# Two key products moved between the transposes ahead of the router, and both key weight halves centred back to back on GpSimd

## What is computed

```python
# layer 0: sigmoid attention
s = einsum('bdn,bdm->bnm', Q, K) / sqrt(dk);  x = x + einsum('bvn,bnm->bvm', V, sigmoid(s))
# layer 0: mixture of 16 experts on y = layernorm(x)
logits = y @ router_weight.T + router_bias          # top 4, softmax, scores
gate_up = einsum('th,ehd->etd', y, gate_up_proj)    # then glu, down_proj, weighted sum
# layer 3: keys of the cross attention, from the context alone
kx, vx = split(einsum('bsi,oi->bso', cond, w_kv_x));  kx = _ln(kx.reshape(b, sc, g, d), kxln_w, kxln_b)
```

## Time and profile before

| | before |
|---|---|
| median of 3 runs (lowest, highest) | 1119.61 us (1118.5, 1120.48) |
| the profiled execution's own time | 1118.99 us |
| its span, first to last instruction | 1117.2 us |
| PE busy | 1016.7 us, 91% |
| DVE busy | 875.7 us, 78% |
| ACT busy | 619.3 us, 55% |
| POOL busy | 571.6 us, 51% |
| mean granted TensorE clock | 0.965 of full speed |

### The profile page before, as it was taken

One profiled execution on the slowest core, in us unless ns is written; L12 is line 12 of the kernel. 1 busy time (PEld: TensorE's weight loads), 2 busy tenths in 40 slices (PEclk: granted clock), 3 DMA queues, 4 the chain that ended last, 5 costly groups with the idle time before them and its releaser, 6 DMA issues.

```text
span 1117.2 us, 18801 instructions
## 1 busy us (share of the span) xinstructions
PE 1016.7 (91%) x6432; PEld 862.2 (77%) x6432; DVE 875.7 (78%) x2156; ACT 619.3 (55%) x1646; POOL 571.6 (51%) x416
## 2 busy tenths in 40 slices
PE   6999999999996899878678999999999999999966
PEld 5458888888885686555456888998889888999955
DVE  6348777767768856598999898888897888888773
ACT  1584444444432345677647667765767676666721
POOL 3146666677552232043346675656555655555550
PEclk9899999999997899898879999999999999999998
DMA  7003111011000011000000101010100000000201
GB/s 263 1 1 109 47 40 57 29 58 57 29 1 27 1 55 54 24 1 1 20 1 20 57 1 38 2 57 1 38 2 27 32 20 20 1 21 1 77 1 38
DMA packets 14719, 37.14 MB, mean 33 GB/s; under 512 B 1488, under 2 KB 6688, under 8 KB 14112
## 3 DMA queue, kind: packets, MB, share of 16 engines
q1 hardware_dynamic: 14624, 35.93, 9.5%
HBM read 34.88 MB, written 1.05 MB: 32 GB/s over the span
## 4 chain that ended last, share of the span: by engine, by line
PE 67%; DVE 19%; ACT 6%; issue 4%; POOL 2%; SPq 1%; DMA 1%; DVEq 0%; ACTq 0%; POOLq 0%
PE bank L725 15%; PE bank L747 8%; PE bank L2129 7%; PE bank L2152 7%; PE bank L2062 7%; PE bank L2037 3%; ACT y L2277 3%; PE bank L2073 3%; PE bank L1101 3%; DVE g_ql L1996 2%; PE bank L2051 1%; PE bank L515 1%; DVE bst L241 1%; PE bank L516 1%; PE bank L1116 1%
## 5 line engine op out<-in xcount | busy, mean ns | idle before, releaser
L2277 ACT ACTIVATE y<-bank,g_mx 128x256 f32<-128x256 f32 x256 | 117.2, 484 | 97.1 <-DVE g_mx L2440 97.1
L2559 POOL TENSOR_TENSOR y<-y,g_sm 128x1024 f32<-128x1024 f32 x64 | 120.1, 1896 | 23.8 <-DVE g_sm L2453 23.8
L2535 POOL TENSOR_TENSOR g_c<-arena 128x1024 fp32r<-128x1024 f32 x30 | 64.0, 2135 | 115.2 <-DVE arena L2374 115.2
L2152 PE MATMUL bank<-arena 128*128 128x256 f32 x512 | 116.1, 380 | 0.0
L776 ACT ACTIVATE arena<-arena 128x512 f32<-128x512 f32 x64 | 40.4, 633 | 120.6 <-DVE arena L861 120.5
L2152 PEld LDWEIGHTS bank<-arena 128*128 128x128 f32 x512 | 95.0, 190 | 11.9 <-issue 0.2
L725 PE MATMUL bank<-b_yh,b_wh 128*128 128x512 f32 x256 | 100.7, 393 | 0.0
L725 PE MATMUL bank<-b_yl,b_wh 128*128 128x512 f32 x256 | 100.0, 391 | 0.0
L725 PE MATMUL bank<-b_yh,b_wl 128*128 128x512 f32 x256 | 99.8, 390 | 0.0
L2037 PE MATMUL bank<-cst,y 128*128 128x128 f32 x512 | 73.3, 275 | 17.6 <-DVE x L2362 14.4
L812 POOL TENSOR_TENSOR b_hl<-arena,b_hh 128x512 fp32r<-128x512 f32 x64 | 81.3, 1291 | 9.6 <-ACT b_hh L785 9.6
(11 more groups left out here) (384 smaller groups left out, 3137.2 us busy)
## 6 DMA issues: line engine op xcount, KB each, us to landing
arena<-in_dram SPq DMA_DIRECT2D x37, 512.0 KB, 3.5
arena<-in_dram SPq DMA_DIRECT2D x17, 256.0 KB, 3.7
arena<-in_dram SPq DMA_DIRECT2D x3, 1024.0 KB, 4.8
arena<-in_dram SPq DMA_DIRECT2D x2, 704.0 KB, 7.2
x<-in_dram SPq DMA_DIRECT2D x4, 256.0 KB, 5.3
cx<-in_dram SPq DMA_DIRECT2D x4, 256.0 KB, 5.3
cxT<-in_dram SPq DMA_DIRECT2D x4, 256.0 KB, 5.9
cx<-in_dram SPq DMA_DIRECT2D x1, 1024.0 KB, 6.9
```

Source lines behind the costliest of these rows:

```text
L2152: m = pe.matmul(o[:, st * 256:st * 256 + 256], g_t[:, c, st * P:st * P + P], keys, start=True, stop=True)
L2277: m = act.activation(g_p[:, c, st, :], o[:, st * 256:st * 256 + 256], ACT.Exp, bias=g_mx[j % 2][:, 2 * c + st:2 * c + st + 1], accum_out=g ...
L2535: pool.tensor_tensor(cat, g_o[j % 2], g_om, ALU.subtract).then_inc(s_gc, 1)
L2559: pool.tensor_tensor(pf, pf, sums, ALU.mult).then_inc(s_gp, 1)
```

## The change

On PE key product 0 now stands between the transposes of batches 0 and 1, and key product 1 between those of batches 1 and 2; logits(0) follows the transposes of batch 2 directly, and the rest of the order stays. On ACT the emptying of key product 0 comes ahead of the copy of batch 2's transposes; the copy of logits(0) moves behind the copy of batch 3, and the rounding of the first expert's weights ahead of the emptying of key product 2. On POOL the two centrings stand back to back, and the root for batch 1 comes behind both. Nothing is computed that was not computed before, and nothing is left out.

```diff
@@ -670,10 +670,12 @@
 
             pe.wait_ge(s_cst, 16)
             pe.wait_ge(s_small, 32)
-            yt_pe(pe, K_B, "B", range(3))
+            yt_pe(pe, K_B, "B", (0,))
+            K_raw_pe(pe, 0)
+            yt_pe(pe, K_B, "B", (1,))
+            K_raw_pe(pe, 1)
+            yt_pe(pe, K_B, "B", (2,))
             logits(0)
-            K_raw_pe(pe, 0)
-            K_raw_pe(pe, 1)
             yt_pe(pe, K_B, "B", (3,))
             K_raw_pe(pe, 2)
             logits(1)
@@ -752,14 +754,15 @@
                 o = take(act, ("B", "lgT", h))
                 empty(act.copy(b_sT[0:NE, h * 512:h * 512 + 512], o[0:NE, :]), ("B", "lgT", h))
 
-            yt_act(act, "B", range(3))
+            yt_act(act, "B", range(2))
+            K_raw_act(act, 0)
+            yt_act(act, "B", (2,))
             split_y_act(act, 0)
-            logits(0)
-            K_raw_act(act, 0)
             K_raw_act(act, 1)
             yt_act(act, "B", (3,))
+            logits(0)
+            split_e_act(act, 0)
             K_raw_act(act, 2)
-            split_e_act(act, 0)
             logits(1)
             K_raw_act(act, 3)
             split_y_act(act, 1)
@@ -2963,9 +2966,8 @@
             ln_pool(pool, C, K_A, EPS)
             ln_pool(pool, C, K_B, EPS, batches=(0,))
             K_centre_pool(pool, 0)
-            ln_pool(pool, C, K_B, EPS, batches=(1,))
             K_centre_pool(pool, 1)
-            ln_pool(pool, C, K_B, EPS, batches=(2, 3))
+            ln_pool(pool, C, K_B, EPS, batches=(1, 2, 3))
             B_pool(pool, C)
             M_pool(pool, C)
             G_pool(pool, C)
```

## The result

The changed kernel takes 1113.87 us (median of 4 runs, 1113.02 to 1114.33) where the kernel before took 1120.05 beside it: ratio 0.9957, 95% interval 0.9942 to 0.9972. Two more sets of the unedited changed kernel gave 1114.2 (ratio 0.9954, 0.9942 to 0.9967) and 1113.35 (0.9948, 0.9935 to 0.9961). Over all sets the median is 1113.84 in 15 runs of it and 1119.55 in 63 of the kernel before: 5.7 us less, where 7.1 were forecast. Seen inside the profile, the opening gained nearly what was forecast, and a part did not reach the end.

A forecast was written before the change was run, and what follows sets the result against it. PE was taken to bound the kernel, by its own line or its waits. Experts starting 7.08 us earlier (40.93 instead of 48.01) gave 1119.61 - 7.1 = 1112.5 us for the median, range 1110.5 to 1116.5.

The forecast's parts named there:

- What bounds it: Opening on PE: busy 1.33 of 5.15 us up to 29.15, then 18.73 of 18.86; work moves from full to empty stretch.
- The three terms on PE: Leaving PE's full stretch: keys 0 and 1, 3.94 us; logits(0) at full clock, 1.64; transposes of batch 2, 0.65.
- POOL: Second centring can run from 21.5 to 23.4 or 23.7 us, before key 0 wants it at 24.55.
- The cover: POOL's root for batch 1 ends at 24.7 us, DVE can use it only at 24.9: wait covered by 0.2.
- DVE: Scaling of batch 1 no longer meets the second centring: 1.87 to 0.70 us, so 1.17 leave DVE's line.
- the two bounds: DVE's adds and statistics under the second centring: nothing gained, or held to 23.7 us, eating the 1.17; zero taken.
- The hand-over: Between POOL's two centrings the waiting DVE scaling goes first: no cost for DVE, about 0.3 us for the second centring.
- the rival in which POOL keeps the port through both: DVE held through both centrings, its line 1.9 us later; gain shrinks to 3.5 us, 1116.0; chance 0.11.
- ACT: New order of copies and emptying keeps up with PE; copy 3 ends at 32.7 us, 0.2 before logits(1) wants it.
- The clock: PE's half clock follows its two waits for y; without them granted clock is 1.00 from 24 to 41 us.
- I find nothing that would take it back: Behind 48.01 us everything starts from the moved events, so the opening's 7.1 us reach the end.
- The slower rival: Moving later work lets more stretches fall to half clock; over 14 us added turns the sign; 1122.5 us, chance 0.05.

The follow-up runs named there:

- changed, second: Changed kernel run again unedited, for a second profile: median 1114.2 us, ratio 0.9954 to the kernel before; experts start at 41.42 us.
- changed, third: Changed kernel run once more unedited, beside two delayed versions of it: 1113.35 us, ratio 0.9948 to the kernel before; experts start at 41.86 us.
- before, second: Kernel before, unedited, profiled a second time: experts start at 48.25 us, and 1069.55 us from there to the end.

## Why the prediction was right

How far each product on PE lies ahead of the same product in the first profile of before, in us, at some times of before (minus: earlier):

```
time in before          85    206    335    390    492    636    718   1055    end
changed               -6.5   -6.5   -6.5   -8.2   -4.7   -5.5   -4.3   -4.2   -4.7
changed, second       -6.6   -6.6   -6.6   -6.1   -3.9   -6.2   -4.9   -4.9   -5.3
changed, third        -6.1   -6.1   -6.1   -6.0   -6.0   -6.0   -6.0   -5.8   -5.9
before, second        +0.2   +0.3   +0.3   +0.4   +0.5   +0.5   +0.6   +0.7   +0.6
```

The lead from the opening passes unchanged through 250 us. In the first profile it then wanders between 8.2 and 4.2, where the clock falls at other moments than in before (0.86 from 334 to 382 us where before has 0.80 from 340 to 390; 0.88 from 432 to 490 where before has 0.94 from 440 to 495; 0.89 from 640 to 655 where before has 1.00); in the third it stays.

- **What bounds it.** Right: PE's full stretch and its empty one. The empty one is full now.
- **The three terms on PE.** Keys 0 and 1 out of the full stretch: right. Logits(0): 1.64 said, 3.52 - 1.82 = 1.70 measured. Transposes of batch 2: 0.65 said and measured. The experts start at 41.53 where 40.93 was said; 0.5 of the 0.6 is the later start of the column sums.
- **POOL.** The second centring ends at 23.80 (23.4 to 23.7 said, with the same 0.5 to add); the root for batch 1 ends at 24.8 and DVE uses it at 25.27. The cover held.
- **DVE.** 1.17 us said for the scaling of batch 1, 1.16 measured. Adds and statistics under a centring cost nothing more, the value taken of the two bounds.
- **The hand-over.** DVE's waiting tile ended 0.15 us behind the first centring (22.05 against 21.90), as taken, so the rival in which POOL keeps the port through both falls. The 0.3 us for POOL's second centring didn't show.
- **ACT.** Copy 3 starts at 32.38, where 32.1 was said, and ends at 33.02; logits(1) starts at 33.57, right behind key 2, so the cover held. The run with ACT's old order puts the price of this part at 1.94 us.
- **The clock.** Said to stay at 2.4 GHz: 1.00 in every slice from 20 to 43 us.
- **The step that was off** is "I find nothing that would take it back". The sum carried the opening's 7.1 to the end; the medians show 5.7, the three profiles 4.7, 5.3 and 5.9. The later start of the column sums accounts for 0.4 to 0.9 of that in the profiles. The longer rest, 1.8, 1.3 and 0.2 us, is the other part. The places where the lead moves are those where the clock differs, but that the clock makes the whole of it is argued and not shown. In the first profile PE was busy for 55.2 us at half clock behind the start of the experts, against 51.9 in before; at half a microsecond for each that gives 1.7 of the 1.8. In the second it was 59.1, which would give 3.6 where 1.3 were lost.
- **The slower rival** was not seen. It asked for 14 us more at half clock behind the opening; the three profiles have 0.4, 3.9 and 0.1 more than the 72.5 of before. The first lost 1.8 us of its lead with nearly the same time at half clock, only at other places; the rival counted the amount alone.
- **What stays open.** Whether the medians lose part of the gain on average, or only by chance: 6.6 us were measured between the medians in the last set, 6.2 and 5.2 in the other two.

## What to carry to other kernels

Where the bounding engine waits and then has a full stretch behind it, independent work moved into the wait counts twice: it leaves the full stretch, and on TensorE it keeps the clock up for what follows (here 3.9 us and 2.3 us of 7.1 in the sum). Such a move needs the engines that feed and empty it reordered with it: without POOL's part or without ACT's part 1.9 us of opening were lost each. An edit of a microsecond is better judged by the distance between two events near it in the profile, which repeated to 0.01 us in the changed kernel, than by a median; but what of it reaches the end only medians tell, and here these were uncertain by a microsecond.

## What the runs showed of the hardware

- Two waits of TensorE with only the 0.6 us of four transposes between them went with a fall of the granted clock to 0.50: in the kernel before waits of 2.17 and 1.65 us, with the fall near 27.5, inside the second; with POOL's order alone 0.99 and 1.66, with the fall near 28.5, just behind the second. With PE's and ACT's order alone waits of 1.29 and 1.60 us with 2.4 us of products between them left it at 1.00. In both kernels in which it fell it came back while PE worked without a gap.
- A VectorE instruction that was held by a GpSimd instruction was not held by the next one, queued directly behind: the scaling of batch 0 took 2.31 us with one centring queued and with two.
- The same program shows a fall of the clock near 640 us in some executions and none in others; the lead shrinks by 1.2 us from 636 to 718 in the first profile of the changed kernel, which has it, and not in the third, which has none.
